# A mixture-of-experts block behind a state-space mixer: x of the last batch in the first one's place, all first weights split early, fc low weights on GpSimd, units assigned ahead of the permutations

## The chip, the cores and the metric

One core of a Trainium2 chip runs the whole program. The metric is the device time of one execution in microseconds. Engines: TensorE (PE in the views, PEld its weight loads, PEq or PEldq its sequencer), VectorE (DVE), ScalarE (ACT), GpSimd (POOL) and SyncE (SP), which only issues DMAs here.

## The reference

Four batches of 512 tokens with 512 features. From `c` six modulation rows per batch are made. Then, shortened:

```python
h = layernorm(x) * (1 + ca) + sa
x = x + ga * mixer(h)            # depthwise conv, projections, selective scan over 512 tokens
h = layernorm(x) * (1 + cb) + sb
top = argmax(softmax(h @ w_router.T))          # one of two experts per token
a = square(where(fc[top] @ h >= 0, h1, 0.5 * h1))
x = x + gb * top_weight * (proj[top] @ a)      # 512 -> 2048 -> 512
```

The router's decision is one sign per token, so the fc and proj products must be close to float32.

## The kernel before

**Two parts.** The first part takes the batches one after the other through layer norm, mixer, residual, the second layer norm and the router. The second part runs the expert layers over all 2048 tokens, sorted by expert: 17 blocks of 128 rows, grouped into five units of 4, 4, 4, 3 and 2 blocks (`UNITS`), and 8 slices `hb` of 256 hidden features.

**Sorting.** For each batch VectorE makes the mask `m1` (which expert), TensorE the prefix counts (`prefix`), VectorE the ranks (`ranks`) and one-hot permutations (`permutations`). TensorE transposes each block of 128 tokens through its permutation (`permuted_block`), so that one expert's tokens come first and the other's last, and the result is written twice: from the front (`place`, ScalarE) and from the back (second copy by ScalarE, for the last batch by VectorE in `place_from_back`). A unit is then a stretch of columns of `XSfull` that has one expert, except the last. Which stretch and which expert is computed from the counts: `assign_first` for units 0 and 1 after three batches, `prepare_rest` and `assign_rest` for units 2 to 4. The engines read the outcome (`startI`, `pickI`) into registers with `value_load`; TensorE's are in `load_unit` (lines 1243 to 1245).

**Float32 from three products.** Weights and activations are split into a high part (`Whi`, `XShi`, `ahi`, a rounding copy on ScalarE) and a low part (`Wlo`, `XSlo`, `alo`, a subtraction), and each product is high by high plus high by low plus low by high (`PARTS`). `split_first` makes the high parts of the first slice's eight weight pieces (four fc, four proj) on ScalarE, `lows` the four fc low parts on VectorE, `low` the four proj low parts on GpSimd. `high_rows(u)` and `low_rows(u)` do it for a unit's tokens.

**The passage between the parts** is what the change is about. On TensorE it is written out by hand: prefix of batch 3, loads of units 0 and 1, `first_fc(0, (0,))` (unit 0, high by high, 8 matmuls), the four permuted blocks of batch 3 (16 transposes), `first_fc(0, (1, 2))` (16 matmuls), `first_fc(1, ...)` (24 matmuls), loads of units 2 to 4, and `proj(0, 0, 0)`, the first proj matmul, which waits for the low activations and for all blocks placed, `s_e0` from the front and `s_e1d` from the back. ScalarE: `place` of batch 2, high rows of units 0 and 1, placing of blocks 0 and 1 of batch 3, proj weights' high parts, and in `job(0, 0, 0, ...)` relu, placing of blocks 2 and 3, and the squares. VectorE: ranks, permutations, low rows of unit 0, four fc low parts, `assign_rest`, low rows of unit 1, two blocks from the back, `twice` (relu(h) + h), two more, `low` (alo).

**Memory.** x of batches 0 to 2 has places of its own in `x_in`; x of batch 3 (`x3`) lies over the second half of `Whi`, so the proj weights' high parts wait until batch 3's residuals are done (line 873 and the line behind it). Its load is issued by SP after mod row 3 (`s_mm` at 4).

```python
            pe.wait_ge(s_e0, KT * NBLK)
            pe.wait_ge(s_e1d, KT * TJ)
            proj(0, 0, 0)
```

## Time and profile before

| | us |
|---|---|
| median of 3 runs | 548.8 (548.78 to 552.28) |
| the profiled execution | 548.64 |
| its span | 546.9 |
| TensorE busy | 508.2 (93%), mean clock 0.974 of full |
| VectorE busy | 351.1 (64%) |
| ScalarE busy | 261.2 (48%) |
| GpSimd busy | 159.4 (29%) |

### The profile page before, as it was taken

To read this page: it belongs to the slowest core of one execution; us is meant where nothing else is said; L and a number is where in the kernel's file an instruction comes from. 1 tells how busy PE (TensorE), PEld (TensorE's weight loads), DVE (VectorE), ACT (ScalarE), POOL (GpSimd) and SP (SyncE) were. 2 spreads that over 40 slices of the span, in tenths; PEclk is the share of its full clock that TensorE was granted. 3 is DMA by queue.
4 is the path that set the end of the run, shared out by engine and by line. 5 is a ranking of instruction groups with operands and counts; after the bars stand their busy time and mean duration, and the time that the engine had idled before them with its cause. 6 is when DMAs were issued, how large, how long until landed. Compare 5 with 4: busy or idle time off the path is not lost.

```text
span 546.9 us, 7697 instructions
## 1 busy us (share of the span) xinstructions
PE 508.2 (93%) x2280; PEld 387.3 (71%) x2280; DVE 351.1 (64%) x734; ACT 261.2 (48%) x520; POOL 159.4 (29%) x204
## 2 busy tenths in 40 slices
PE   7899899999398999999999999999999999999990
PEld 1354355545276888898888888888888888988880
DVE  4688999898998675464445354545454544668781
ACT  2763387946786743443443344344346334433220
POOL 1100003030334520330150033034004304868583
PEclk9999999999778999999999999999999999999995
DMA  8930442220042004030022022002102300467692
GB/s 297 427 126 0 139 171 77 78 78 1 2 135 99 4 3 156 20 136 2 1 78 79 1 78 79 1 1 91 67 1 78 117 1 4 115 120 179 81 164 96
DMA packets 15729, 46.29 MB, mean 85 GB/s; under 512 B 5223, under 2 KB 5223, under 8 KB 12344
## 3 DMA queue, kind: packets, MB, share of 16 engines
q1 hardware_dynamic: 10600, 34.71, 17.8%
q0 software_dynamic: 5072, 10.79, 9.5%
q8 instruction: 40, 0.66, 0.5%
q14 instruction: 17, 0.14, 0.1%
HBM read 37.30 MB, written 8.71 MB: 84 GB/s over the span
## 4 chain that ended last, share of the span: by engine, by line
PE 71%; DVE 18%; issue 4%; ACT 3%; DMA 1%; DVEq 1%; POOL 1%; ACTq 0%; SPq 0%; POOLq 0%
PE bank L1200 34%; PE bank L1169 32%; DVE xc L1327 4%; DVE res L1365 2%; DVE st L1372 1%; PE bank L992 1%; DMA x_in<-x 1%; DVE st L1309 1%; ACT XSfull L769 1%; DVE eabs L1389 1%; DVE hs L1355 1%; PE bank L1006 1%; PE bank L1016 1%; DVE XSfull L1607 1%; PE bank L1033 1%
## 5 line engine op out<-in xcount | busy, mean ns | idle before, releaser
L565 POOL TENSOR_TENSOR Wlo<-raw,Whi (+1 forms) x60 | 76.3, 1301 | 227.7 <-ACT Whi L911 219.1
L1630 DVE TENSOR_TENSOR acc<-acc,bank 128x512 f32<-128x512 f32 x110 | 74.9, 687 | 57.2 <-PE bank L1200 57.2
L1614 DVE TENSOR_TENSOR twice_h<-twice_h,bank 128x512 f32<-128x512 f32 (+2 forms) x80 | 48.2, 606 | 95.5 <-ACT twice_h L882 95.5
L1169 PE MATMUL bank<-XShi,Wlo 128*128 x304 | 108.1, 355 | 0.0
L1169 PE MATMUL bank<-XSlo,Whi 128*128 x304 | 108.0, 355 | 0.0
L1169 PE MATMUL bank<-XShi,Whi 128*128 x304 | 108.0, 355 | 0.0
L1200 PE MATMUL bank<-Whi,ahi 128*128 128x512 f32 x268 | 105.2, 393 | 2.1 <-DVE alo L1620 2.1
L1200 PE MATMUL bank<-Wlo,ahi 128*128 128x512 f32 x268 | 105.2, 393 | 0.0
L1200 PE MATMUL bank<-Whi,alo 128*128 128x512 f32 x268 | 104.9, 392 | 0.0
L891 ACT ACTIVATE ahi<-twice_h 128x512 fp32r<-128x512 f32 (+2 forms) x78 | 44.6, 572 | 118.9 <-PE bank L1200 118.9
L882 ACT ACTIVATE twice_h<-bank 128x512 f32<-128x512 f32 (+2 forms) x78 | 41.4, 534 | 85.5 <-PE bank L1169 76.2
L1169 PEld LDWEIGHTS bank<-XSlo,Whi 128*128 128x128 f32 x304 | 57.3, 189 | 7.5
L1169 PEld LDWEIGHTS bank<-XShi,Whi 128*128 128x128 f32 x304 | 57.3, 188 | 7.5
L1169 PEld LDWEIGHTS bank<-XShi,Wlo 128*128 128x128 f32 x304 | 57.3, 189 | 6.9
L1200 PEld LDWEIGHTS bank<-Whi,ahi 128*128 128x128 f32 x268 | 50.6, 189 | 12.8 <-issue 2.5
L1200 PEld LDWEIGHTS bank<-Whi,alo 128*128 128x128 f32 x268 | 50.7, 189 | 10.8
L1200 PEld LDWEIGHTS bank<-Wlo,ahi 128*128 128x128 f32 x268 | 50.8, 189 | 10.1
L1620 DVE TENSOR_TENSOR alo<-a_full,ahi 128x512 fp32r<-128x512 f32 (+2 forms) x78 | 45.4, 612 | 0.0
L892 ACT ACTIVATE a_full<-twice_h 128x512 f32<-128x512 f32 (+2 forms) x78 | 43.4, 556 | 0.0
L1327 DVE SCALAR_TENSOR_TENSOR xc<-hT,cw,xc 128x512 f32<-128x512 f32 x48 | 33.6, 743 | 1.8 <-ACT xc L699 1.4
L769 ACT ACTIVATE XSfull<-bank,cols 128x128 f32 (+1 forms) x64 | 24.1, 457 | 17.0 <-PE bank L1061 15.4
L911 ACT ACTIVATE Whi<-raw 128x512 fp32r<-128x512 f32 x56 | 30.5, 616 | 0.0
(197 smaller groups left out, 579.1 us busy)
## 6 DMA issues: line engine op xcount, KB each, us to landing
raw<-wffn SPq DMA_DIRECT2D x16, 1024.0 KB, 5.2
wm<-wmod SPq DMA_DIRECT2D x6, 1024.0 KB, 12.8
out<-res SPq DMA_DIRECT2D x4, 1024.0 KB, 4.5
x_in<-x SPq DMA_DIRECT2D x3, 1024.0 KB, 12.3
ga_bc<-ga_rows SPq DMA_DIRECT2D x4, 256.0 KB, 3.6
x<-x SPq DMA_DIRECT2D x1, 1024.0 KB, 5.3
bc<-router_rows_scaled SPq DMA_DIRECT2D x4, 256.0 KB, 3.6
wx_sb<-wx SPq DMA_DIRECT2D x1, 514.0 KB, 8.5
```

Source lines behind the costliest of these rows:

```text
L565: pool.tensor_tensor(Wlo[:, hb % 2, c, :], raw[:, c, :], Whi[:, hb % 2, c, :].bitcast(F32), ALU.subtract).then_inc(s_wlo, 1)
L769: act.activation(XSfull[:, k, bass.ds(first, P)], place_bank[b][j][:, P * k:P * k + P], ACT.Identity, bias=cols[:, 4, k, b:b + 1], scale=c ...
L882: act.activation(twice_h[:, m, 0:w], hP[(par + u) % 2][m][:, 0:w], ACT.Relu).then_inc(s_relu[m], 1)
L891: act.activation(ahi[:, m, 0:w], twice_h[:, m, 0:w], ACT.Square, scale=0.5).then_inc(s_ah[m], 1)
L892: act.activation(a_full[:, m, 0:w], twice_h[:, m, 0:w], ACT.Square, scale=0.5).then_inc(s_af[m], 1)
L911: act.activation(Whi[:, 1 - par, c, :], raw[:, c, :], ACT.Copy).then_inc(s_whi, 1)
L1169: mm = pe.matmul(hP[(par + u) % 2][m][:, c0:c1], W[wp][:, par, 2 * e + k // 2, o:o + P], XS[xp][:, k, bass.ds(start_row[u] + c0, c1 - c0)] ...
L1200: mm = pe.matmul(yP[bank_of[s]][:, :], ahl[ap][:, m, P * s:P * s + P], W[wp][:, par, 4 + 2 * experts[s] + m, :], start=(m == 0 and n == 0) ...
L1327: ins = dve.scalar_tensor_tensor(xc[:, b % 2, k, :], hT[b % 2][:, k, tap:tap + L], cw[:, k, tap:tap + 1], xc[:, b % 2, k, :], ALU.mult, AL ...
L1614: dve.tensor_tensor(twice_h[:, m, 0:w], twice_h[:, m, 0:w], hP[(par + u) % 2][m][:, 0:w], ALU.add).then_inc(s_q2[m], 1)
L1620: dve.tensor_tensor(alo[:, m, 0:w], a_full[:, m, 0:w], ahi[:, m, 0:w].bitcast(F32), ALU.subtract).then_inc(s_al2[m], 1)
L1630: dve.tensor_tensor(acc[:, n, :], acc[:, n, :], yP[s][:, :], ALU.add).then_inc(s_yu, 1)
```

## The change

1. `x_row` and `load_x`: x of batch 3 goes to `x_in[:, 0]`, batch 0's place, once batch 0's residuals are done (SP waits for `s_x2` at 4). `x3` is gone.
2. ScalarE: `split_first` makes all eight high parts ahead of batch 2's placing; three blocks of batch 2 are placed ahead of `guess2(3)`, and three of batch 3 ahead of unit 0's job. High rows wait for batch 3's residuals.
3. `prepare_rest` moves from VectorE to GpSimd, which signals `s_limits`. Behind it GpSimd makes the four fc low parts, between the position step of batch 2 and its scatters, after batch 3's first residual and products. `lows` on VectorE is gone. The proj low parts now wait for the low rows of units 0 and 1.
4. VectorE: unit and offset registers are loaded early, `assign_rest` stands ahead of `permutations`; one block is placed from the back ahead of `twice`, one behind it, two behind `low`. Gap and top weight of the last batch go from unit 0 to unit 1.
5. TensorE: `keep_rate`, three float32 matmuls of 512 columns into a free bank, stands ahead of batch 3's prefix and waits for its first margin product. The loads of units 2 to 4 move from behind unit 1's fc matmuls to between the first eight and the permuted blocks.

```diff
-            return x_in[:, b, j, :] if b < XRING else x3[:, j, :]
+            return x_in[:, b % XRING, j, :]
...
-            sp.wait_ge(s_mm, 4)
+            sp.wait_ge(s_x2, TJ)
             load_x(3)
...
+            def prepare_rest():
+                pool.wait_ge(s_early, 2)
+                own.link(pool.tensor_scalar(rows_in_front[:, :], ends[:, 1:2], float(P), None, ALU.mult))
+                own.mark(pool.tensor_scalar(basis[:, 0:NU - 2], basis[:, 0:NU - 2], rows_in_front[:, 0:1], None, ALU.add))
+                own.link(pool.tensor_scalar(limits[:, :], blkF[:, 0:LEFT], rows_in_front[:, 0:1], None, ALU.add))
+                pool.tensor_scalar(limits[:, :], limits[:, :], -1.0, float(TOK), ALU.mult, ALU.add).then_inc(s_limits, 1)
...
+                if b == NB - 2:
+                    prepare_rest()
+                    pool.wait_ge(s_x2, TJ * (NB - 1) + 1)
+                    pool.wait_ge(s_pb, 2 * NB)
+                    pool.wait_ge(s_cv, KT * NB)
+                    for c in range(CH // 2):
+                        low(0, c)
                 if b == NB - 1:
+                    pool.wait_ge(s_xlo, KT * 2)
                     pool.wait_ge(s_wlo, CH // 2)
...
-            split_first(range(4))
-            place(2, (0, 1))
+            split_first(range(CH))
+            place(2, (0, 1, 2))
             guess2(3)
-            place(2, (2, 3))
+            place(2, (3,))
...
+            act.wait_ge(s_x2, TJ * NB)
             high_rows(0)
             high_rows(1)
             margin_exp(3)
-            place(NB - 1, (0, 1))
-            act.wait_ge(s_x2, TJ * NB)
-            split_first(range(4, CH))
+            place(NB - 1, (0, 1, 2))
...
-                    job(0, 0, 0, ((place, (NB - 1, (2, 3))),))
+                    job(0, 0, 0, ((place, (NB - 1, (3,))),))
...
+            def keep_rate():
+                pe.wait_ge(s_q, TJ * (NB - 1) + 1)
+                pe.wait_ge(s_hm, NB)
+                for n in range(3):
+                    pe.matmul(pC[:, :], ident[:, :], wout_sb[:, :], start=True, stop=True)
             def prefix(b):
+                if b == NB - 1:
+                    keep_rate()
...
             first_fc(0, (0,))
+            pe.wait_ge(s_unit, 2)
+            for u in range(2, NU):
+                load_unit(u)
+            pick.append(pe.value_load(pickI[0:1, NU:NU + 1], min_val=0, max_val=2))
             for j in range(TJ):
                 permuted_block(NB - 1, j)
             first_fc(0, (1, 2))
             pe.wait_ge(s_x2, TJ * NB)
             first_fc(1, (0, 1, 2))
-            pe.wait_ge(s_unit, 2)
-            for u in range(2, NU):
-                load_unit(u)
-            pick.append(pe.value_load(pickI[0:1, NU:NU + 1], min_val=0, max_val=2))
             proj_weights_ready(0)
...
-                    if b == NB - 1:
-                        prepare_rest()
...
+            dve.wait_ge(s_early, 2)
+            first_rows = [first_row(u) for u in range(2)]
             ranks(NB - 1)
+            assign_rest()
             permutations(NB - 1)
-            low_rows(0)
-            lows(range(4))
-            assign_rest()
-            low_rows(1)
+            dve.wait_ge(s_off, NB)
+            low_rows(0, first_rows[0])
+            first = [first_place(j) for j in range(2)]
+            low_rows(1, first_rows[1])
+            first += [first_place(j) for j in range(2, TJ)]
             dve.wait_ge(s_e1, TJ * (NB - 1))
             for u in range(NU):
                 if u == 0:
-                    place_from_back(0)
-                    place_from_back(1)
+                    place_from_back(0, first[0])
                 twice(0, 0, u)
                 if u == 0:
-                    place_from_back(2)
-                    place_from_back(3)
+                    place_from_back(1, first[1])
                 elif u + 1 < NU:
-                    low_rows(u + 1)
+                    if u == 1:
+                        dve.wait_ge(s_unit, 2)
+                    low_rows(u + 1, first_row(u + 1))
                 if u > 0:
                     accumulate("first", 0, u - 1)
                 low(0, u)
                 if u == 0:
+                    place_from_back(2, first[2])
+                    place_from_back(3, first[3])
+                if u == 1:
```

How the instructions stand now, at three places. The rows have line number, operation, and output from inputs; a number behind a name tells apart tiles of one name.

TensorE, before, behind unit 0's first fc matmuls (the row with XShi and Whi is their end, for one of the two experts):

```order
L1148 MATMUL bank<-XShi,Whi 128x512
L1148 ISA
L1148 MATMUL bank<-XShi,Whi 128x512 x5
L1156 UNCONDITIONAL_BRANCH
L1061 MATMUL bank<-perm,z_71 128x128 x16
L1154 COMPARE_AND_BRANCH
L1148 ISA
```

TensorE, after, the same place, from the third of the seven loads on (two more stand ahead in the same form; ISA rows are register steps):

```order
L1270 TENSOR_LOAD startI
L1270 ISA x2
L1271 TENSOR_LOAD pickI
L1271 ISA x2
L1270 TENSOR_LOAD startI
L1270 ISA x2
L1271 TENSOR_LOAD pickI
L1271 ISA x2
L1284 TENSOR_LOAD pickI
L1284 ISA x2
L1087 MATMUL bank<-perm,z_71 128x128 x16
```

The seven loads have come between the fc matmuls and the 16 transposes of the permuted blocks (z by perm).

VectorE, before, behind the low rows of unit 0:

```order
L1596 TENSOR_TENSOR XSlo<-XSfull,XShi 128x512
L1494 TENSOR_TENSOR Wlo<-raw,Whi 128x512 x4
L1459 TENSOR_SCALAR begun<-limits,run 128x8
L1460 TENSOR_TENSOR change<-change,begun 128x56
L1462 TENSOR_REDUCE assignment<-change 128x7
L1463 TENSOR_TENSOR startI<-assignment,basis 128x3
L1464 TENSOR_TENSOR pickI<-assignment,basis 128x4
L1593 TENSOR_LOAD startI
```

VectorE, after, behind batch 3's ranks:

```order
L1443 TENSOR_TENSOR rank<-excl,bank 128x4
L1478 TENSOR_SCALAR begun<-limits,run 128x8
L1479 TENSOR_TENSOR change<-change,begun 128x56
L1481 TENSOR_REDUCE assignment<-change 128x7
L1482 TENSOR_TENSOR startI<-assignment,basis 128x3
L1483 TENSOR_TENSOR pickI<-assignment,basis 128x4
L1448 TENSOR_SCALAR perm<-colidx,place_col 128x128 x4
L1610 ISA
L1610 TENSOR_TENSOR XSlo<-XSfull,XShi 128x512
```

The five instructions of the assignment (begun to pickI) now stand ahead of the permutations, and the four fc low parts (Wlo) are gone from VectorE.

VectorE, before, around unit 0's alo:

```order
L1607 ISA
L1607 TENSOR_SCALAR XSfull<-bank,cols 128x128
L1620 TENSOR_TENSOR alo<-a_full,ahi 128x512 x2
L1698 TENSOR_SCALAR n0f<-run 128x1
L1699 TENSOR_SCALAR gapI<-tokF,n0f 128x1
```

VectorE, after, around the same instructions:

```order
L1623 TENSOR_SCALAR XSfull<-bank,cols 128x128
L1636 TENSOR_TENSOR alo<-a_full,ahi 128x512 x2
L1623 ISA
L1623 TENSOR_SCALAR XSfull<-bank,cols 128x128
L1623 ISA
L1623 TENSOR_SCALAR XSfull<-bank,cols 128x128
L1623 ISA
```

Eight instructions that place blocks 2 and 3 from the back (XSfull from a bank) have gone from ahead of alo to behind it; the piece shows the first three of them.

## Rows read from the trace of the kernel before

**Rows 1.** Chain of waits in order of time: start us, us, what

```profile
167.39 1.23 DVE alo L1620 x2
```

**Rows 2.** TensorE's timeline: start us, us, engine line op out<-in count [idle before <-releaser]

```profile
147.99 0.58 PE L1042 MATMUL bank<-m,before 128*128 128x4 f32 x2 [6.60 <-DVE m L1403]
...
151.41 3.78 PE L1148 MATMUL bank<-XShi,Whi 128*128 x8 [2.41 <-ACT XShi L859]
154.98 2.84 PE L1061 MATMUL bank<-perm,z 128*128 128x128 f32 x16
157.57 2.08 PE L1148 MATMUL bank<-XSlo,Whi 128*128 x8
...
161.30 1.98 PE L1148 MATMUL bank<-XShi,Whi 128*128 x8
...
169.03 0.50 PE L1200 MATMUL bank<-Whi,ahi 128*128 128x512 f32 x1 [2.12 <-DVE alo L1620]
```

**Rows 3.** TensorE by stretch: us, busy us (count), granted clock, DMA share, GB/s

```profile
141.40:148.00 6.60, 0.01 (x1) 0.64 0.01 0
...
151.40:155.00 3.60, 3.59 (x9) 0.50 0.01 2
155.00:158.00 3.00, 3.00 (x19) 0.69 0.26 35
...
169.03:176.30 7.27, 7.27 (x25) 0.77 0.10 32
```

**Rows 4.** DMA issues by line: KB each, us from issue to landing

```profile
x<-x SPq DMA_DIRECT2D x1, 1024.0 KB, 5.3
```

**Rows 5.** Timeline of VectorE and the SP queue from 59 to 72 us

```profile
59.44 0.68 DVE L1365 TENSOR_TENSOR res<-bank,x_in 128x512 f32<-128x512 f32 x1
...
62.78 0.27 SPq L462 DMA_DIRECT2D router_rows_scaled<-wd_row  x1
...
71.18 0.69 DVE L1389 CUSTOM_DVE_ANT_0 eabs<-res,bc 128x512 f32<-128x512 f32 x1
```

**Rows 6.** ScalarE's timeline from 136 to 166 us

```profile
136.70 1.51 ACT L769 ACTIVATE XSfull<-bank,cols 128x128 f32 x4 [2.48 <-PE bank L1061]
...
149.55 4.27 ACT L859 ACTIVATE XShi<-XSfull  x8 [0.80 <-ACT XSfull L773]
...
159.25 2.20 ACT L748 ACTIVATE Whi<-raw 128x512 fp32r<-128x512 f32 x4
...
162.60 1.51 ACT L769 ACTIVATE XSfull<-bank,cols 128x128 f32 x4 [0.17 <-issue]
```

**Rows 7.** VectorE's timeline from 136 to 168 us

```profile
136.22 0.12 DVE L1452 TENSOR_SCALAR rows_in_front<-ends 128x1 f32<-128x1 f32 x1
...
136.98 0.69 DVE L1365 TENSOR_TENSOR res<-bank,x 128x512 f32<-128x512 f32 x1
...
143.03 0.69 DVE L1389 CUSTOM_DVE_ANT_0 xc<-res,bc 128x512 f32<-128x512 f32 x1
...
147.76 0.17 DVE L1403 TENSOR_SCALAR m<-lg 128x4 f32<-128x4 f32 x1
...
150.71 0.87 DVE L1422 TENSOR_SCALAR perm<-colidx,place_col 128x128 f32<-128x128 f32 x4
...
156.45 0.22 DVE L1459 TENSOR_SCALAR begun<-limits,run 128x8 f32<-128x8 f32 x1
...
166.02 1.37 DVE L1607 TENSOR_SCALAR XSfull<-bank,cols 128x128 f32 x4 [0.22 <-ACT XSfull L769]
```

**Rows 8.** Timeline of GpSimd and VectorE: the two kinds of subtraction

```profile
160.04 5.36 POOL L565 TENSOR_TENSOR Wlo<-raw,Whi 128x512 fp32r<-128x512 f32 x4 [8.61 <-ACT Whi L748]
...
193.49 1.51 DVE L1596 TENSOR_TENSOR XSlo<-XSfull,XShi  x1
```

**Rows 9.** TensorE's sequencer: loads of unit registers, ns min/median/max, first to last start

```profile
L1244 PEldq TENSOR_LOAD <-startI x2: 309/397/485, 148.0 to 149.5; - x2
...
L1244 PEldq TENSOR_LOAD <-startI x3: 297/300/307, 162.9 to 165.6; - x3
```

More of the change, by code:

```diff
@@ L174, in build @@
         x_in = take("x_in", [P, XRING, TJ, DM])
-        x3 = at("x3", [P, TJ, DM], F32, o_whi + ZB)
         def x_row(b, j):
-            return x_in[:, b, j, :] if b < XRING else x3[:, j, :]
+            return x_in[:, b % XRING, j, :]
         eabs = take("eabs", [P, L])
@@ L401, in build @@
         s_early = sem("first_units_assigned")
+        s_limits = sem("limits_ready")
         s_unit = sem("units_assigned")
@@ L435, in load_x @@
             def load_x(b):
-                sp.dma_start(x_in[:, b] if b < XRING else x3[:, :, :], x[b]).then_inc(s_x[b], 16)
+                sp.dma_start(x_in[:, b % XRING], x[b]).then_inc(s_x[b], 16)
             sp.dma_start(c_sb[:, :], cT).then_inc(s_c, 16)
@@ L1447, in assign_first @@
                 dve.tensor_copy(startI[:, 0:2], startf[:, :]).then_inc(s_early, 1)
-            def prepare_rest():
-                own.link(dve.tensor_scalar(rows_in_front[:, :], ends[:, 1:2], float(P), None, ALU.mult))
-                own.mark(dve.tensor_scalar(basis[:, 0:NU - 2], basis[:, 0:NU - 2], rows_in_front[:, 0:1], None, ALU.add))
-                own.link(dve.tensor_scalar(limits[:, :], blkF[:, 0:LEFT], rows_in_front[:, 0:1], None, ALU.add))
-                own.link(dve.tensor_scalar(limits[:, :], limits[:, :], -1.0, float(TOK), ALU.mult, ALU.add))
             def assign_rest():
                 dve.wait_ge(s_change, CHANGES)
+                dve.wait_ge(s_limits, 1)
                 own.link(dve.tensor_scalar(begun[:, :], limits[:, :], run[:, 0:1], None, ALU.is_gt))
@@ L1489, in out_weights @@
                 dve.tensor_tensor(woutg[b][:, :], wout_sb[:, :], ga_bc[:, b, :], ALU.mult).then_inc(s_wg, 1)
-            def lows(cs):
-                for c in cs:
-                    dve.wait_ge(s_whi, c + 1)
-                    dve.tensor_tensor(Wlo[:, 0, c, :], raw[:, c, :], Whi[:, 0, c, :].bitcast(F32), ALU.subtract).then_inc(s_wlo, 1)
             own.mark(dve.memset(ones[:, :], 1.0))
@@ L1591, in _, with first_row, low_rows @@
                 margins(b)
-            def low_rows(u):
-                start_row = dve.value_load(startI[0:1, u:u + 1], min_val=0, max_val=ROWS - P * UNITS[u])
+            def first_row(u):
+                return dve.value_load(startI[0:1, u:u + 1], min_val=0, max_val=ROWS - P * UNITS[u])
+            def low_rows(u, start_row):
                 for k in range(KT):
@@ L1597, in low_rows, with first_place, place_from_back @@
                                       XShi[:, k, bass.ds(start_row, P * UNITS[u])].bitcast(F32), ALU.subtract).then_inc(s_xlo, 1)
-            def place_from_back(j):
+            def first_place(j):
+                return dve.value_load(offI[0:1, (NB - 1) % 2, j:j + 1], min_val=0, max_val=P * (TJ * (NB - 1) + j))
+            def place_from_back(j, first):
                 b = NB - 1
                 n = TJ * b + j
-                first = dve.value_load(offI[0:1, b % 2, j:j + 1], min_val=0, max_val=P * n)
                 dve.wait_ge(s_e0, KT * (n + 1))
```

## The prediction

> **What bounds the kernel now.** I read the chain of waits in order of time first, then the timeline of each engine over the stretch in which the chain changes engine, the granted clock there, and last the records of TensorE's sequencer. From the first proj matmul at 169.03 us on, the chain is TensorE alone until the end, matmul behind matmul; the wait ahead of that matmul is on VectorE's last step of alo, which ends at 168.62 [rows 1, 2]. So the kernel is two parts: up to 169.03 us a relay between engines, and behind it some 360 us in which nothing of the change reaches TensorE. The change's worth is how far the first proj matmul moves, plus what the clock then does.
>
> In the relay TensorE has little to do from 141.4 to 151.4: 0.01 us busy between 141.4 and 148.0, at a mean granted clock of 0.64 [rows 3]. It runs the first eight fc matmuls (high by high) from 151.41 at the low level, 0.50, that is 1.2 GHz, at (154.98 - 151.41)/8 = 0.45 us each; from 157.57 the same shape takes 2.08 us for eight, 0.24 to 0.26 each, at 2.4 GHz [rows 2, 3].
>
> **The change, part by part.**
>
> *x of batch 3 loaded later.* Its issue moves from behind mod row 3 to when the last residual of batch 0 is written, 60.1 us. The transfer took 5.3 us [rows 4], so it lands near 65.4. The risk is behind it: the small store of the router rows is issued at 62.78 on the same queue, and its broadcasts are first read at 71.18 [rows 5]. If the store waits for the whole transfer, everything behind it is late by 65.4 - 62.8 = 2.6 us. Price: bounds 0 and +2.6; I take 0, since between 62.8 and 71.2 a store, four broadcasts of 256 KB (a quarter of the 5.3 us each) and their starts leave some 2 us over.
>
> *Eight splits on ScalarE ahead of batch 2's placing.* Four of them (2.2 us, the row at 159.25) move to about 134. ScalarE waited 2.48 us there for TensorE's block, ending at 136.70 [rows 6], so they fit to 0.2 us. One more block of batch 2 goes ahead of the rsqrt guess; the guess comes perhaps 0.9 us later and VectorE's four margin products cover that. The high rows of unit 0 then start near 148.0 instead of 149.55. This gains nothing by itself: TensorE starts the fc matmuls at 151.41, 1.2 us after the first high part is ready, because its own sequencer is late (below). If that cover were gone it would be worth 1.5 us.
>
> *prepare_rest off VectorE.* VectorE was busy without a gap from 136.22 to the mask at 147.76. Four instructions go: 136.98 - 136.22 = 0.76 us [rows 7]. Against it, GpSimd now makes the four low parts of the fc weights in this stretch: prepare_rest on GpSimd is about 1.5 us from 136.0, then 5.3 us (the row at 160.04) until 142.9. The margin products, two SBUF inputs, would start at 142.3. Row: an XSlo subtraction of 256 columns, also two SBUF inputs, took 1.51 us beside GpSimd's subtraction, where its sisters take 0.4 [rows 8]. So the overlap of 0.6 us costs between 0 and 1.1; I take 0.3. (The other unknown is whether row statistics, one SBUF input, are slowed too; no row shows it.) The mask comes 0.46 us earlier, near 147.3.
>
> The GPSIMD Engine Reference of the Trainium skill, section Specifications, says that GpSimd's SBUF interfaces are shared with VectorE and contend with instructions in a 2-port mode or with two SBUF inputs. The row at 193.49 agrees. By that rule the residuals (one PSUM input) beside GpSimd cost nothing.
>
> *keep_rate.* Three more float32 matmuls, two passes each, wait for the first margin product near 143.0. At 0.43 us a pass (the column count of the fc matmuls, float32 at full clock) they take 2.6 us, at the low clock 5.1. The clock fell about 1.85 us after 141.4, with TensorE idle (a mean of 0.64 over 6.6 us) [rows 3], so at 143.2, just when they start. At worst they end at 148.1 and hold the prefix products by 0.7 us; at best they leave the full clock for what follows. I take neither: a gap of 3 us behind the prefix remains.
>
> *The loads of units 2 to 4.* This is the term that decides. On TensorE's sequencer the four register loads of units 0 and 1 begin with the prefix: a start register at 148.0 and the next at 149.5, a pick between, so 0.75 us each. With the branch that is why the fc matmuls start 3.4 us after the prefix products, whatever ScalarE does. The loads of units 2 to 4 stand at 162.9 to 165.6 for the three starts, four loads apart: 0.67 us each [rows 9]. Before, they stand behind all fc matmuls of unit 1 and run while the array works these off; they are over by 167.7, ahead of the wait that ends at 169.03: they cost nothing. Now all seven (three starts, three picks, one more pick) stand between the first eight fc matmuls and the permuted blocks. Fc starts at 147.3 + 0.2 + 3.4 = 150.9. Its eight matmuls are handed over in about 1.0 us (bounds 0.6 and 3.5, the time they run), the units are assigned by then (ranks and 1.0 us of assign_rest end near 151.2), and 7 x 0.67 = 4.7 us of loads follow, 0.1 of it beside the hand-over: the first permuted block at 156.5, where it was at 154.98. That is +1.5 us, and the array is idle for 2.2 us ahead of it. By the slower loads, 0.75 each, it is 157.2.
>
> *Assignment ahead of the permutations* puts 1.0 us between the ranks and the permutation columns on VectorE: they start at 151.0 instead of 150.71 (1.0 us for the five instructions from 156.45, less the 0.46 and the time of the ranks as before) [rows 7], and end long before 156.5. Covered. If the loads cost nothing, this would be what TensorE waits for. The low rows of unit 0 and 1 are ready by 156.8, and VectorE has lost the 2.5 us of fc low parts.
>
> *Blocks and low products at which clock.* Before, the clock rose within 155 to 158 us (mean 0.69), some 5 us after TensorE began to work without a gap. The gap of 2.2 us now breaks that run. After the gap of 2.1 us ahead of 169.03 the clock was down for about 3.3 of the next 7.3 us (mean 0.77) [rows 3]. So I take the low level until about 160.5: 16 block transposes 2.8 us instead of 2.6 (to 159.3), then 16 fc matmuls, about three of them at 0.43: 3.7 + 0.5 to 163.5. Before it was 161.3 [rows 2]. So +2.2 us.
>
> *From the end of unit 0's fc to the first proj matmul.* Before: 161.3 to 169.03, 7.7 us. Relu 1.1; ScalarE's two placed blocks 3.1 with the gap (1.51 each, from 162.60 [rows 6]); four squares of 0.52; last alo. Now one block is placed between (1.6 less on ScalarE): last square at +4.5, alo at +5.2. But VectorE places blocks 2 and 3 from the back behind alo, and TensorE still waits for all sixteen of these pieces: two rows like the one at 166.02 [rows 7], 1.37 each with 0.22 between, to +8.0, and 0.4 to the matmul: 8.4. That is +0.7 us, since what saves ScalarE a block is given back on VectorE.
>
> *Behind it.* The dip of the clock behind the wait comes again; it may be shorter or longer, by -0.5 to +1. Batch 3's scatters start some 12 us later on GpSimd and the next low parts end near 200 instead of 195; they are needed at 204. Covered.
>
> Sum: to the end of unit 0's fc +2.2 (the -0.46 of the mask is in it), and +0.7: +2.9, with 0.1 for the open ends: +3.0. The profiled execution took 548.64 us, 1.74 more than its span; its median sister runs are 548.8. Forecast 548.8 + 3.0 = 551.8 us.
>
> **Rivals.**
>
> A. *The loads are hidden and the clock is kept.* If the loads ran beside the array's work, blocks would start with the permutations at 152.6 at full clock, the low products would be paced by the low rows and end near 158.4, and proj would start at 166.8: -2.2, so 546.6 us. For it: the loads of units 2 to 4 were hidden before. Against it: there 16 to 24 matmuls were queued ahead, here eight, and the blocks stand behind the loads in the same queue.
>
> B. *Slower by over 1%: the clock stays low through all of unit 0's fc.* keep_rate at the low clock and the new gap leave TensorE at 1.2 GHz until proj: 16 x 0.43 = 6.8 instead of 3.7 us, blocks 2.8, so unit 0's fc ends at 166.1, +4.8, and with 0.7 proj starts 5.5 us late: 554.3 us. It decides from the point where the low level lasts beyond 163 us. Against it: the clock rose 5 us after work began, before.
>
> C. *The two cancel.* The loads cost +1.5, but keep_rate brings the first fc matmuls and the blocks to full clock, alo ends earlier, and the trailing places are 0.7: about +1, 549.8 us.
>
> The Trainium skill (TensorE: Matmul & The Clock Gate, section Why this matters for your kernels) asks for no long idle gaps between bursts of matmuls, which speaks against C and for B; the gap of 2.1 us ahead of 169.03 brought a fall here, so the trace agrees.
>
> **How the numbers follow.** Forecast 0.58, A 0.15, B 0.09, C 0.18. The range reaches from A to B: 546.6 to 554.4. A measurement tells about 1% (5.5 us) from no change. Only the far side of B and an unlooked-for wait in the relay give slower: 0.08. Faster by 5.5 us would need more than A: 0.02. Within 1%: 0.90.
>
> **What would show it.** TensorE's records: seven loads between the first fc matmuls and the blocks, at 0.67 us, an idle gap of about 2 us, the first block at about 156.5, the low products at about 159.3, first proj at about 172, waiting on VectorE's placed block and not on alo. The mask 0.4 to 0.8 us earlier. I am wrong if blocks start before 154.5, if the gap ahead of proj ends on alo, or if the mask comes later than 147.8.

## The result, and the profile after

The changed kernel takes 559.76 us (median of 4 runs, 559.29 to 559.86), the kernel before beside it 548.85 us. The ratio is 1.018, with a 95% interval of 1.0143 to 1.0218 (the quotient of the medians alone is 1.020; one of the 4 runs before took 552.28 us). The forecast was 551.8 us in a range up to 554.4: the kernel is slower by more than any of the cases allowed. Slower is clear of the noise; whether by 2% is not. The profiled run took 559.86 us with a span of 558.0 us, 11.1 more than the 546.9 of before.

The waits of TensorE in the changed kernel, from 140 to 240 us; columns: what it waited for, us in total, times, longest:

```profile
PE bank L1226 <- DVE alo L1636: 6.1, 1, 6.1
PE bank L1226 <- DVE XSfull L1623: 3.4, 1, 3.4
PE bank L1087 <- issue: 3.2, 2, 1.6
PE bank L1174 <- ACT XShi L877: 3.1, 1, 3.1
...
```

The last three are the ones that the prediction speaks of. The first is new and the largest, and it isn't in the relay at all. TensorE's timeline shows where it stands (`...` marks rows left out, here and below):

```profile
147.72 0.28 PE L1068 MATMUL bank<-m,before 128*128 128x4 f32 x2
...
151.28 3.57 PE L1174 MATMUL bank<-XShi,Whi 128*128 x8 [3.06 <-ACT XShi L877]
156.46 1.94 PE L1087 MATMUL bank<-perm,z 128*128 128x128 f32 x16 [1.61 <-issue]
158.16 2.09 PE L1174 MATMUL bank<-XSlo,Whi 128*128 x8
...
170.91 0.50 PE L1226 MATMUL bank<-Whi,ahi 128*128 128x512 f32 x1 [3.39 <-DVE XSfull L1623]
...
199.46 0.80 PE L1226 MATMUL bank<-Whi,ahi 128*128 128x512 f32 x1 [6.12 <-DVE alo L1636]
```

Up to 170.91 this is the relay of [rows 2] with the loads in it: the first fc matmuls start 0.1 us earlier than before, the blocks 1.5 us later, unit 0's fc ends 0.6 us later and proj starts 1.9 us later. At 199.46 stands the 6.1 us wait, where the kernel before works without a gap. The chain of waits in the same place (start, us, what):

```profile
183.71 5.44 PE bank L1226 x24
189.15 4.20 PE bank L1195 x24
194.34 1.02 ACT XShi L877 x3
195.46 2.90 issue
198.36 0.69 DVE alo L1636
199.46 8.64 PE bank L1226 x24
```

Two readings. The 24 proj matmuls behind the wait take 8.64 us where the same 24 at 183.71 take 5.44: the granted clock fell in the wait and was 0.50 from 196 to 205 us, at the cost of 3.2 us. And "195.46 2.90 issue" misleads: the chain finds no semaphore that VectorE's second alo waited for, and calls the time issue. What VectorE did in it is in the timelines of VectorE and GpSimd, by start and duration:

```profile
189.79 9.24 DVE L1636 TENSOR_TENSOR alo<-a_full,ahi 128x512 fp32r<-128x512 f32 x2
```

```profile
181.62 1.02 POOL L600 DMA_INDIRECT sorted_rows<-meta,posI  x1 [19.63 <-issue]
...
186.83 1.10 POOL L604 DMA_INDIRECT sorted_rows<-gap,gapI  x1 [0.30 <-issue]
187.96 9.93 POOL L574 TENSOR_TENSOR Wlo<-raw,Whi  x8
```

GpSimd subtracts the low parts of the next eight fc weights in one run, 187.96 to 197.89. The first alo of unit 2 starts inside it, at 189.79, and ends behind it. By tile it took 8.64 us, and the second, from 198.36 on, the usual 0.68 (durations in ns, least, median, most, then the first and the last start; the pieces of GpSimd in the second fence):

```profile
L1636 DVE TENSOR_TENSOR alo<-a_full,ahi x2: 679/4661/8643, 189.8 to 198.4; 128x512 fp32r<-128x512 f32 x2
```

```profile
L574 POOL TENSOR_TENSOR Wlo<-raw,Whi x8: 1252/1268/1302, 188.0 to 196.6; - x8
```

An instruction that takes 8.64 us for work of 0.68 stood still for 8 of them. I read it as kept from its operands by GpSimd, which the runs below test. The profile counts it as busy: no idle time of VectorE points at it, only the mean of one instruction does. In the kernel before the same tiles stand otherwise (VectorE, then GpSimd):

```profile
168.53 0.15 DVE L1698 TENSOR_SCALAR n0f<-run 128x1 f32<-128x1 f32 x1
...
187.95 1.33 DVE L1620 TENSOR_TENSOR alo<-a_full,ahi 128x512 fp32r<-128x512 f32 x2
```

```profile
169.98 1.02 POOL L582 DMA_INDIRECT sorted_rows<-meta,posI  x1 [4.59 <-issue]
...
178.61 5.06 POOL L565 TENSOR_TENSOR Wlo<-raw,Whi  x4 [2.38 <-ACT Whi L911]
189.47 5.24 POOL L565 TENSOR_TENSOR Wlo<-raw,Whi  x4 [5.80 <-ACT Whi L911]
```

There GpSimd keeps step with ScalarE's splits in two groups of four, and unit 2's alo falls into the pause between them. The change takes the gap's position and the top weight (n0f, gapI, den and the reciprocal) from unit 0 to unit 1 on VectorE, from 168.53 to 180.16:

```profile
180.16 0.15 DVE L1722 TENSOR_SCALAR n0f<-run 128x1 f32<-128x1 f32 x1
```

GpSimd's scatters of batch 3 wait for them and start 11.6 us later, at 181.62. It comes to the first four subtractions so late (187.96) that ScalarE's second four splits are done, at 192.49, before it has worked the first four off (near 193.0); nothing paces it any more, and the run of eight covers alo. ScalarE's splits in the changed kernel:

```profile
179.43 2.18 ACT L928 ACTIVATE Whi<-raw 128x512 fp32r<-128x512 f32 x4
...
190.31 2.18 ACT L928 ACTIVATE Whi<-raw 128x512 fp32r<-128x512 f32 x4
```

So the 11.1 us are 1.9 in the relay (170.91 - 169.03, of which 0.3 is no work of the change: the residual that stands in [rows 5] at 59.44 is at 59.72 here, ahead of the first edited step), 6.1 of waiting, 3.2 of lower clock behind it: 11.2.

### The profile page after: what moved, and what is told of

Same layout as the page of the kernel before. It is cut to its first block, busy times and chain, and to the rows that moved or that the text cites. A ratio compares the mean times of both kernels' runs of the same rounds, so it can differ in the third digit from the quotient of the medians.

```text
span 558.0 us, 7714 instructions
## 1 busy us (share of the span) xinstructions
PE 514.8 (92%) x2286; PEld 389.4 (70%) x2286; DVE 354.8 (64%) x726; ACT 261.0 (47%) x520; POOL 165.4 (30%) x212
## 4 chain that ended last, share of the span: by engine, by line
PE 72%; DVE 16%; issue 4%; ACT 4%; DMA 1%; POOL 1%; DVEq 0%; ACTq 0%; SPq 0%; POOLq 0%
PE bank L1226 34%; PE bank L1195 32%; DVE xc L1353 4%; DVE res L1391 2%; DVE st L1398 1%; DMA x_in<-x 1%; PE bank L1009 1%; ACT XSfull L787 1%; PE bank L1050 1%; PE bank L1054 1%; DVE st L1335 1%; DVE eabs L1415 1%; PE bank L1023 1%; PE bank L1033 1%; PE bank L1174 1%
## 5 line engine op out<-in xcount | busy, mean ns | idle before, releaser
L574 POOL TENSOR_TENSOR Wlo<-raw,Whi (+1 forms) x64 | 80.5, 1288 | 225.0 <-ACT Whi L928 218.9
L1226 PE MATMUL bank<-Whi,ahi 128*128 128x512 f32 x268 | 106.6, 398 | 9.5 <-DVE alo L1636 6.1
L1636 DVE TENSOR_TENSOR alo<-a_full,ahi 128x512 fp32r<-128x512 f32 (+2 forms) x78 | 53.4, 714 | 0.7 <-ACT a_full L909 0.7
```

Source lines behind the costliest of these rows:

```text
L574: pool.tensor_tensor(Wlo[:, hb % 2, c, :], raw[:, c, :], Whi[:, hb % 2, c, :].bitcast(F32), ALU.subtract).then_inc(s_wlo, 1)
L1226: mm = pe.matmul(yP[bank_of[s]][:, :], ahl[ap][:, m, P * s:P * s + P], W[wp][:, par, 4 + 2 * experts[s] + m, :], start=(m == 0 and n == 0) ...
L1636: dve.tensor_tensor(alo[:, m, 0:w], a_full[:, m, 0:w], ahi[:, m, 0:w].bitcast(F32), ALU.subtract).then_inc(s_al2[m], 1)
```

## The experiments

Theory: the stall is contention of VectorE's subtraction of two SBUF inputs with GpSimd's run, and the move of four small instructions causes it by its effect on GpSimd's order in time. Rival: the loads on TensorE's sequencer and the places from the back (the terms of the forecast) cost more than priced, and the late wait is their sequel. Each run's kernel is compared with the kernel before, run beside it on the same chip, and the ratio of the two is given with its 95% interval. The kernel before had medians of 549.2 to 550.5 us there, so the ratios say more than the times. Places in the traces are from the profiled execution alone.

**f1: those four instructions back at unit 0** (with one line changed, the `if` over them).

```diff
 changed kernel, VectorE, first slice
-                if u == 1:
+                if u == 0:
                     own.link(dve.tensor_scalar(n0f[:, :], ...
```

> Changed kernel, with VectorE's gap and top weight of the last batch back at unit 0 (behind the two blocks placed from the back). Theory S (starvation): GpSimd's scatters then start near 171.5 us, its two groups of low parts of slice 1 (four subtractions each) run apart again, and no alo of 512 columns overlaps them: both alo of unit 2 take 0.69 us, the 6.1 us wait of TensorE and the low clock behind it (3.1 us) go: 559.8 - 9.2 = 550.6 us, between 549.5 and 551.5. Rival T (VectorE is only late, by its extra work in unit 1 and the reordered relay): the long alo stays at 5 us or more and the time stays above 556 us.

Measured: 553.02 us against 550.45, 1.0035 (1.0005 to 1.0065). The wait on alo is gone; unit 2's alo (190.09) again stands ahead of GpSimd's second group (191.61):

```profile
190.09 1.33 DVE L1636 TENSOR_TENSOR alo<-a_full,ahi 128x512 fp32r<-128x512 f32 x2
```

```profile
180.75 5.05 POOL L574 TENSOR_TENSOR Wlo<-raw,Whi  x4 [0.67 <-ACT Whi L928]
191.61 5.24 POOL L574 TENSOR_TENSOR Wlo<-raw,Whi  x4 [5.81 <-ACT Whi L928]
```

One line moved back gives 1.45% of the 1.8%. The time is above the expected 549.5 to 551.5, but so is the kernel before on this chip (550.45 for 548.85); the ratio gives 550.8. What remains, 0.35% or 1.9 us (2.6 by the medians), is the part that the prediction had priced (at 3.0).

The two profiled executions lie 7.7 us apart and not the 9.3 of the stall, because the relay differs too: f1's first proj matmul came at 172.83, 1.9 us later than in the changed kernel, with the blocks at the low level of the clock (3.65 us) where the changed kernel has 1.94.

**f2: the kernel before with only this move.**

```diff
 kernel before, VectorE, first slice
-                if u == 0:
+                if u == 1:
                     own.link(dve.tensor_scalar(n0f[:, :], ...
```

> Kernel before, with only the gap and top weight of the last batch moved from unit 0 to unit 1, nothing else of the change. Theory S: scatters start near 179.5 us instead of 170, the low parts of slice 1 run as one piece from 186 to 196, the first alo of unit 2 (start 188) lasts until that piece ends, 7 to 9 us, TensorE waits about 6 us and runs 3 us at the low clock behind: 548.8 + 9 = 557.8 us (556.5 to 559). Rival T: within 0.5 us of before, 548.8.

Measured: 559.22 us against 550.45, 1.0127 (1.0069 to 1.0185); the ratio gives 7.0 us and the medians 8.8, of the 9 expected. Nothing else of the change is in it, and the same run of eight and the same stall are there:

```profile
186.78 9.94 POOL L565 TENSOR_TENSOR Wlo<-raw,Whi  x8
```

```profile
190.04 7.83 DVE L1620 TENSOR_TENSOR alo<-a_full,ahi 128x512 fp32r<-128x512 f32 x2
```

TensorE waited 6.1 us for it. With f1 this makes the move both enough and needed: the rival falls. The stall here began 1.4 us later than in the changed kernel relative to the end of GpSimd's run (190.04 to 196.72), and was shorter by as much (7.83 instead of 9.24 for the two, 7.23 for the first): its length is what is left of the run, not a property of the subtraction.

**f3: GpSimd waits for each of its own subtractions before the next.**

```diff
 changed kernel, GpSimd
-            with pool.Fori(1, NHB - 1) as hb:
+            for c in range(CH):
+                pool.wait_ge(s_wlo, CH + c)
+                low(1, c)
+            with pool.Fori(2, NHB - 1) as hb:
```

> Changed kernel, with a wait of GpSimd on its own previous subtraction ahead of each of the eight low parts of slice 1; they still run at the same time beside alo, but no longer back to back. If a VectorE instruction with two SBUF inputs gets in only at a pause of GpSimd (theory S), the wait opens one every 1.3 us: the alo of unit 2 takes at most 2 us each, TensorE's wait shrinks from 6.1 us to under 1: 551 to 553 us. Rival U (the two engines share the port in time, in proportion): GpSimd is as busy as before, the alo stays at 7 to 9 us and the time at 559 to 560.

Measured: 555.82 us, 1.0079 (1.005 to 1.0109), above the 551 to 553 expected (553.2 by the ratio), with the alo as short as expected. The eight pieces start 1.38 to 1.77 us apart and cover 190.85 to 202.67, longer than before, and yet the alo that start in them pass:

```profile
190.85 11.82 POOL L574 TENSOR_TENSOR Wlo<-raw,Whi 128x512 fp32r<-128x512 f32 x8
```

```profile
193.47 2.39 DVE L1639 TENSOR_TENSOR alo<-a_full,ahi 128x512 fp32r<-128x512 f32 x2
...
197.57 5.39 DVE L1613 TENSOR_TENSOR XSlo<-XSfull,XShi  x4 [0.21 <-ACT XShi L880]
```

The first alo took 0.68 and the second 1.79 us; each of the four XSlo took 1.1 to 1.5 us, the time from one of GpSimd's pieces to the next: one VectorE instruction gets in at each pause. It is not free (four XSlo take 5.39 us instead of the 2.85 at the same place in the kernel before), and TensorE is idle for 1.3 us ahead of an fc matmul behind them. The profiled execution also has a fall of the clock behind the first proj matmul (0.50 from 176 to 178 us) that f1's has not.

**h12: f3's eight subtractions written out, without its waits.** f3 differs from the changed kernel in two things, the waits and the loop written out; this one has the second alone.

```diff
 changed kernel, GpSimd
-            with pool.Fori(1, NHB - 1) as hb:
+            for c in range(CH):
+                low(1, c)
+            with pool.Fori(2, NHB - 1) as hb:
```

> The changed kernel with slice 1's eight low subtractions written out on GpSimd ahead of the loop, as in the run f3, but without f3's waits between them. It tells which of f3's two differences from the changed kernel let VectorE in. Theory (the waits did: GpSimd's queue runs empty for a moment): written out alone, the run stays one piece of 9.9 to 10.1 us, the first alo of unit 2 takes 7 to 9 us, TensorE waits 5 to 6 us on it, and the ratio to the kernel before stays 1.014 to 1.022. Rival (the loop does it, its instructions being ready in advance): alo takes 2 us or less as in f3 and the ratio is 1.003 to 1.010.

Measured: 560.86 us, 1.0216 (1.018 to 1.0251), with the stall to the nanosecond:

```profile
189.50 9.92 POOL L574 TENSOR_TENSOR Wlo<-raw,Whi 128x512 fp32r<-128x512 f32 x8
```

```profile
L1638 DVE TENSOR_TENSOR alo<-a_full,ahi x2: 679/4660/8642, 191.3 to 199.9; 128x512 fp32r<-128x512 f32 x2
```

So it is the waits, that is GpSimd pausing between two of its instructions, that let VectorE in.

**f4: f1 with the loads of units 2 to 4 back behind unit 1's fc matmuls.**

```diff
 f1, TensorE
             first_fc(0, (0,))
-            pe.wait_ge(s_unit, 2)
-            for u in range(2, NU):
-                load_unit(u)
-            pick.append(pe.value_load(pickI[0:1, NU:NU + 1], min_val=0, max_val=2))
             for j in range(TJ):
                 permuted_block(NB - 1, j)
             first_fc(0, (1, 2))
             first_fc(1, (0, 1, 2))
+            pe.wait_ge(s_unit, 2)
+            for u in range(2, NU):
+                load_unit(u)
+            pick.append(pe.value_load(pickI[0:1, NU:NU + 1], min_val=0, max_val=2))
             proj_weights_ready(0)
```

> The run with gap and top weight back at unit 0, and TensorE's loads of units 2 to 4 back behind unit 1's fc matmuls as well. My reading of the records: seven loads of 0.67 us hold the permuted blocks from about 154.9 to 156.5; without them the blocks start near 153 to 154.9 and the first proj matmul 1.5 to 3 us earlier: that run minus 1.5 to 3, about 548.5 us. Rival: the loads were hidden and the permutations or the two blocks placed last set the time: the same as that run within 0.5.

Measured: 551.06 us, 1.0013 (0.9989 to 1.0037): 0.2% or 1.2 us less than f1 (2.0 by the medians, on the same chip), with intervals that overlap. Counted from batch 3's prefix the blocks start 1.9 us earlier than in f1 (6.9 instead of 8.8), most of it the loads, and the first proj matmul comes 3.8 us earlier (21.3 instead of 25.1), since here the blocks ran at the full level (1.91 us) and in f1 at the low one (3.65). But 2.7 of the 3.8 is given back: from that matmul to the end f4 needs 380.2 us and f1 377.5, since the clock is at 0.62 from 167 to 170 us and 0.50 from 170 to 173, behind a wait of 3.3. f1 had nearly the same wait, 3.1, and no fall. The wait in both ends on VectorE's last placed block.

**g5: f1 without keep_rate.**

```diff
 f1, TensorE
             def prefix(b):
-                if b == NB - 1:
-                    keep_rate()
```

> The changed kernel with the gap and top weight back at unit 0 (as in the run f1, 1.0035 of the kernel before) and without keep_rate's three matmuls. Theory: TensorE then has nothing to do from about 141.4 to the prefix near 147.5, the first fc matmuls and the blocks still run at the low level (they did in f1 too, blocks 3.65 us), so the ratio to the kernel before stays within 0.1% of f1's: 1.0025 to 1.0045. Rival (keep_rate is worth its place): the low level lasts longer, through the blocks and eight more fc matmuls, and the first proj matmul comes 1 to 2 us later: 1.006 to 1.007. Second rival (keep_rate costs, since its last matmul ends 1 us or less before the prefix): 0.5 us less, 1.002 to 1.003.

Measured: 552.21 us, 1.0043 (1.0019 to 1.0068), against f1's 1.0035 (1.0005 to 1.0065): no difference. The prefix alone ran slower without it (0.59 and 0.57 us for its two rows, 0.28 and 0.36 in f1); the first fc matmuls (3.78 for eight) and the blocks (3.65) take what they take in f1.

**g6: f1 with blocks 2 and 3 from the back ahead of alo.**

```diff
 f1, VectorE, unit 0
                     place_from_back(1, first[1])
+                    place_from_back(2, first[2])
+                    place_from_back(3, first[3])
 ...
                 low(0, u)
-                if u == 0:
-                    place_from_back(2, first[2])
-                    place_from_back(3, first[3])
```

> The kernel of f1 with batch 3's blocks 2 and 3 placed from the back on VectorE ahead of unit 0's low part of alo instead of behind it. Theory (behind unit 0's fc TensorE waits for VectorE's trailing places and for nothing else): the wait ahead of the first proj matmul ends on alo and is near 0.5 us instead of 3.1, the first proj matmul is 2.5 us earlier, ratio to the kernel before 0.998 to 1.000. Rival (ScalarE's squares and its one placed block decide, so that alo itself ends late): the wait ends on alo but at nearly the same time, gain under 1 us, ratio 1.002 or more.

Measured: 549.9 us, 1.0012 (0.9986 to 1.0037), between the forecast (up to 1.000) and the rival (from 1.002). The wait ahead of proj now ends on alo and is 2.5 us, not the 0.5 expected:

```profile
172.92 0.50 PE L1226 MATMUL bank<-Whi,ahi 128*128 128x512 f32 x1 [2.51 <-DVE alo L1636]
```

```profile
165.55 1.29 DVE L1630 TENSOR_TENSOR twice_h<-twice_h,bank 128x512 f32<-128x512 f32 x2 [2.34 <-ACT twice_h L899]
166.75 1.36 DVE L1623 TENSOR_SCALAR XSfull<-bank,cols 128x128 f32 x4
168.33 1.37 DVE L1623 TENSOR_SCALAR XSfull<-bank,cols 128x128 f32 x4 [0.22 <-DVE XSfull L1623]
169.91 1.37 DVE L1623 TENSOR_SCALAR XSfull<-bank,cols 128x128 f32 x4 [0.22 <-DVE XSfull L1623]
171.19 1.29 DVE L1636 TENSOR_TENSOR alo<-a_full,ahi 128x512 fp32r<-128x512 f32 x2
```

Three blocks in a row now stand ahead of alo. The order of places and alo changed the wait by 0.6 us (3.1 in f1), since both must be done before proj. Ahead of its twice step VectorE is idle for 2.3 us; h9 uses that. On g5's chip, where both ran, g6 is 2.3 us faster by the medians, but its profiled blocks ran at the full level (1.94) and g5's at the low one (3.65), so the order alone is not shown to give this.

**g7: g6 with the loads back as in f4.**

> The kernel of g6 with the loads of units 2 to 4 back behind unit 1's fc matmuls, as in the kernel before. Theory (the three terms add): the loads are worth another 1.0 to 1.3 us as between f1 and f4, so the first proj matmul is about 3 us earlier than in the kernel before relative to batch 3's prefix, and the fall of the clock behind the wait goes too: ratio 0.994 to 0.997, faster than both kernels. Rival (the terms share one slack: with the blocks earlier, alo and not the blocks decides, and it does not move with the loads): the same as g6 within 0.1%.

Measured: 547.52 us, 0.9962 (0.9937 to 0.9988). It beats both kernels, and g6 on the same chip by 0.5%, so the rival, that alo doesn't move with the loads, falls. But half of the expectation is missed: the first proj matmul is not 3 us earlier than in the kernel before. Counted from the prefix it comes at 21.7 us, before at 21.0. What g7 has is the part behind it, from the first proj matmul to the end: 376.2 us (545.8 - 169.59), with no fall of the clock behind the wait, where the kernel before needs 377.9 with one.

**g8: g7 without keep_rate.**

> The kernel of g7 without keep_rate. If keep_rate does nothing: the same as g7 within 0.1%. If it is what brings the blocks to the full level once the loads are out of their way: blocks take 2.8 us or more instead of 1.9 and the time is 1 us longer, 0.2% above g7.

Measured: 547.96 us, 0.996 (0.9934 to 0.9985), the same as g7; the blocks take 3.04 us with keep_rate out and 2.96 with it. Here too its matmuls give nothing.

**h9: g7 with the order of the kernel before on VectorE.**

```diff
 g7, VectorE, unit 0
                 if u == 0:
                     place_from_back(0, first[0])
+                    place_from_back(1, first[1])
                 twice(0, 0, u)
                 if u == 0:
-                    place_from_back(1, first[1])
                     place_from_back(2, first[2])
                     place_from_back(3, first[3])
```

> The kernel of g7 with VectorE's blocks from the back in the order of the kernel before: blocks 0 and 1 ahead of unit 0's twice steps, 2 and 3 between these and alo. In g7 VectorE was idle for 2.3 us ahead of its twice step and alo then stood behind three blocks. Theory (VectorE's row of places is what alo waits for, ScalarE's last square ends 1.4 us before alo starts): the second block moves into the idle stretch, alo starts 1.4 us earlier and TensorE's wait ahead of proj falls from 2.0 to about 0.8 us; ratio 0.9915 to 0.9945 of the kernel before. Rival (ScalarE's squares decide; they themselves wait for VectorE's twice step, which the second block delays): within 0.1% of g7, 0.995 to 0.997.

Measured: 547.43 us, 0.9956 (0.994 to 0.9971), beside g7 once more (run h11) at 0.9975 (0.9955 to 0.9995) on the same chip. alo starts at 166.72 and ends at 168.0; the last fc matmul of unit 1 ends at 168.03. TensorE waits for no engine any more there:

```profile
169.29 0.50 PE L1226 MATMUL bank<-Whi,ahi 128*128 128x512 f32 x1 [1.26 <-issue]
```

The gain over g7 is 0.2%, with intervals that overlap, and the ratio is above the 0.9915 to 0.9945 expected. Counted from the prefix, alo starts 1.5 us earlier than in h11 (18.0 instead of 19.5), as expected, but the first proj matmul only 0.7 us earlier (20.6 instead of 21.2): 1.26 us on TensorE's own sequencer are what is left, where the last of the seven register loads starts only at 168.0.

The run h11 is g7's kernel unchanged:

> The kernel of g7 once more, beside h9 on the same chip, so that the two can be compared: 0.994 to 0.998 of the kernel before, as g7 gave 0.9962.

**h10: h9 with prepare_rest and the fc low weights back on VectorE.**

```diff
 h9, GpSimd, behind positions(2)
-                    prepare_rest()
-                    for c in range(CH // 2):
-                        low(0, c)
 h9, VectorE
                     top_weight(b - 1)
+                    if b == NB - 1:
+                        prepare_rest()
 ...
             low_rows(0, first_rows[0])
+            lows(range(4))
 ...
```

> The kernel of h9 with prepare_rest and the four fc low weights of slice 0 back on VectorE (prepare_rest behind top_weight, the low weights behind unit 0's low rows). Theory (they cost 0.76 us ahead of the mask and 2.5 us in front of the low rows of unit 1, which then hold TensorE's blocks and low products only in part, since TensorE has other products there): 0.5 to 1 us longer than h9, 0.1 to 0.2%. Rival (this part of the change is what brings the gain, the low rows of unit 1 come too late and the places from the back behind them): 2.5 to 3.3 us longer, 0.5 to 0.6%. Second rival (all hidden): the same.

Measured: 547.39 us, 0.9965 (0.9953 to 0.9978): the same as h9. The second rival holds. VectorE's places begin 1.2 us later (159.97 instead of 158.79; 2.1 us later counted from batch 2's last block), but there was slack for that ahead of its twice step. The mask is as late as in the kernel before (7.0 us behind batch 2's last block; 6.3 in h9), and keep_rate, at the low level of the clock (5.49 us for its six passes), holds the prefix until 149.41, 1.3 us behind the mask. Neither shows in the time.

## Why the prediction was wrong

**The step that failed** is one sentence under "Behind it": batch 3's scatters start some 12 us later on GpSimd, the next low parts end near 200 instead of 195, they are needed at 204, "Covered". What it says of GpSimd came true (scatters 11.6 later, low parts done at 197.9 and so before 204), and TensorE never waited for a low part of a weight. The step asked only who waits for GpSimd's result. It did not ask who works beside GpSimd in the stretch into which its work moves. That was VectorE with a subtraction of two SBUF inputs, on which proj waits: it took 8.64 us instead of 0.68, TensorE waited 6.1 us for it and lost 3.2 us more at the low clock, 9.3 us for a term priced at nothing. f1 and f2 show that the move brings it, f3 and h12 that GpSimd's run without a pause does.

**The price was mis-sized as well, in the place where it was seen.** [rows 8] show an XSlo of 1.51 us beside GpSimd's subtraction, and the prediction took it as a slow-down of at most 1.1 us per overlap. That instruction had waited for the end of the run as well; it only came at the last piece (193.25 to 194.72). The bound from it holds only where GpSimd has one piece left. With seven left it is 8.0 us (8.64 - 0.68). It was also charged to one stretch of the program, not to each in which the two now meet.

The page SBUF — State Buffer of the Trainium skill, section SBUF: two separate sides, says that VectorE and GpSimd share a port pair as an exclusive lock: the one that starts first has it for its whole instruction, and the other is blocked. The trace agrees that nothing is shared in proportion, but not on the length: the blocked alo sat through seven instructions of GpSimd of 1.25 us each, where that rule, read for one instruction, gives 1.3 us at most. In f3, with a pause between them, it got in behind one.

Point by point otherwise:

- **x of batch 3.** Right at 0. The transfer was issued at 60.43, and the first product that reads the broadcasts started at 71.47 against 71.18 [rows 5], which is the 0.3 us that the whole run is late.
- **Splits on ScalarE.** The place was right: 132.33 to 136.58, the placing at 136.99 instead of 136.70 [rows 6]. The high rows started at 148.91, not near 148.0; the first fc matmuls started at 151.28, forecast 150.9.
- **prepare_rest and the mask.** The mask came at 147.34 instead of 147.76 [rows 7], -0.42 where -0.46 was forecast. That this is so near is luck: the 0.3 us taken for contention did not come, and the whole run was 0.3 us late instead. GpSimd's low parts ended at 142.66 and the first margin product started at 142.60, so the overlap was 0.06 us, not 0.6. Row statistics, with one SBUF input, took their 0.69 us beside GpSimd's run.
- **keep_rate.** Right at nothing (g5, g8). Its prices hold too: six passes took 2.84 us at the full level (g6) and 5.49 at the low one (h10), for the 2.6 and 5.1 forecast.
- **The loads.** Right in place and mechanism: the blocks started at 156.46, forecast 156.5, with 1.6 us of idle array where 2.2 were forecast. What they are worth in the end is 1.2 us between f1 and f4 and 2.7 between g6 and g7, by the ratios.
- **The clock at the blocks.** Wrong in this run: the blocks took 1.94 us at the full level, not 2.8, and unit 0's fc ended at 161.9, not 163.5. In f1, f3 and h12, the same up to here, they took 3.65 at the low level, and in f1 unit 0's fc ended at 164.1. It varied between runs of like kernels by 1.7 us, and nothing here tells by what. The prediction took the fall behind the wait as sure to come again; f2 had the same wait of 2.1 us without a fall.
- **From there to proj.** Right in kind: the wait ended on VectorE's last placed block (it ended at 170.2) and proj came at 170.91, forecast about 172. From the end of unit 0's fc it took 9.0 us, not 8.4. So the 1.9 us of the relay, for the 3.0 forecast, are two terms that were off in opposite directions: 0.6 for the 2.2 up to the end of unit 0's fc, and 1.3 for the 0.7 behind it.
- **Rivals.** None had the stall. Of their conditions, A's hidden loads fell (the blocks came 1.5 us later), B's low level did not last to the end of unit 0's fc in any run, and C's blocks at the full level came true in this run, with proj at +1.9 and not +1; f1, with keep_rate too, had them at the low one. The prediction for the rest of the change stands near f1: 1.9 us measured (0.3 to 3.6), 3.0 forecast.

f1 still loses 1.9 us, and g7 (twice), h9 and h10 gain 1.4 to 2.4. The profiled executions show where (us; "block" is the start of the last block of batch 2 on TensorE, ahead of the whole relay):

| kernel | block | first proj matmul | between | from there to the end |
|---|---|---|---|---|
| before | 140.76 | 169.03 | 28.3 | 377.9 |
| changed | 141.04 | 170.91 | 29.9 | 387.1 |
| f1 | 141.07 | 172.83 | 31.8 | 377.5 |
| g7 | 141.25 | 169.59 | 28.3 | 376.2 |
| h9 | 142.05 | 169.29 | 27.2 | 376.9 |
| h10 | 141.10 | 168.58 | 27.5 | 376.9 |

With the loads and the places put back, the relay is shorter than before by 1 us at most, and g7's gain lies behind it, where the kernel before had a fall of the clock in this execution. The earlier mask and the low parts on GpSimd are not the source, since h10 has neither. Which of the remaining steps is, no run isolates.

## What to carry to other kernels

When a change moves work of GpSimd in time, by its own order or by what it waits for, lay VectorE's instructions with two SBUF inputs over the stretch that it moves into: each that starts while GpSimd runs back to back may last until GpSimd pauses. A wait that paces GpSimd by another engine is then worth having. And when a profile shows one duration out of line with its sisters, take it for a wait, and bound it by what it waited for, not by what it happened to cost.

## What the runs showed of the hardware

- A VectorE subtraction of two SBUF inputs that starts inside a run of GpSimd subtractions took 8.64 us (changed kernel and h12) and 7.23 (f2) instead of 0.68, each ending 0.5 us behind the run. GpSimd's pieces are hardly touched meanwhile: 1.25 to 1.30 us.
- VectorE's copies from PSUM (187.15 to 189.88 in the changed kernel, 2.73 for four, three of them beside the same run) took hardly longer than without it (2.63 in f1). Beside GpSimd's four subtractions from 137.70 to 142.66, VectorE's TENSOR_TENSOR with one PSUM and one SBUF input (the residual) took 0.67 us, as ever. So it is not the operation; of the forms seen here only two SBUF inputs were held up.
- With a wait between GpSimd's instructions (f3) their starts lie 1.39 us apart instead of 1.25 where no VectorE subtraction comes, and one gets in at each pause where they do.
- One thing stays open. In the kernel before, an XSlo that started at 192.82, inside the group of four, took 0.75 us: it got in between the third piece and the fourth (which took 1.47 instead of 1.29), with no wait known there. In the run of eight no alo did.
- Around waits ahead of proj, the clock fell with 2.1 us (before), 3.1 (f3), 3.3 (f4), 3.4 (changed kernel) and 6.1 (changed kernel, f2, h12), and did not with 2.0 (g7), 2.1 (f2), 2.2 (h10), 2.5 (g6) and 3.1 (f1, g5, h12). 2.1 and 3.1 stand on both sides: the length of the wait alone does not tell it.
